# Routed token rows loaded in 32-token blocks and turned by VectorE instead of TensorE

## The reference

```python
sort_idx = jnp.argsort(sel_flat)
xs = x_exp[sort_idx]
group_sizes = jnp.bincount(sel_flat, length=E).astype(jnp.int32)
g = jax.lax.ragged_dot(xs, w_gate, group_sizes)
u = jax.lax.ragged_dot(xs, w_up, group_sizes)
d = jax.lax.ragged_dot(jax.nn.silu(g) * u, w_down, group_sizes)
...
out = d[unsort_idx].reshape(T, K, H)
expert_out = jnp.sum(out * weights[..., None], axis=1)
shared = jax.nn.silu(x @ sw_gate) * (x @ sw_up) @ sw_down
```

## Time and profile before

| what | us |
|---|---|
| median of 3 runs | 2290.17 (2286.09 to 2292.93) |
| span of the profiled execution | 2293.4 |
| TensorE busy | 1971.3 (86%) |
| VectorE busy | 1182.9 (52%) |
| ScalarE busy | 565.1 (25%) |
| GpSimd busy | 1116.9 (49%) |

### The profile page before, as it was taken

One profiled execution on the slowest core, in us unless ns is written; L12 is line 12 of the kernel. 1 busy time (PEld: TensorE's weight loads), 2 busy tenths in 40 slices (PEclk: granted clock), 3 DMA queues, 4 the chain that ended last, 5 costly groups with the idle time before them and its releaser, 6 DMA issues. The chain is left out here.

```text
span 2293.4 us, 33594 instructions
## 1 busy us (share of the span) xinstructions
PE 1971.3 (86%) x10564; PEld 1441.9 (63%) x10565; DVE 1182.9 (52%) x2230; ACT 565.1 (25%) x1164; POOL 1116.9 (49%) x552
## 2 busy tenths in 40 slices
PE   5956887968896689998799999999999999997991
PEld 3423443743343233333599989999999999996880
DVE  2554443557776767774774335444444455443330
ACT  3320222401114345443222212121212121211110
POOL 0000000003457356564044558666666788777886
PEclk9977998888996789999899999999999999998995
DMA  3043101402225366711135445545445555654999
GB/s 116 0 112 105 46 27 44 158 32 85 83 71 186 133 213 211 230 52 43 40 105 182 170 142 165 168 151 170 154 150 167 183 163 178 193 165 118 209 202 211
DMA packets 199487, 305.98 MB, mean 133 GB/s; under 512 B 16472, under 2 KB 94808, under 8 KB 199416
## 3 DMA queue, kind: packets, MB, share of 16 engines
q1 hardware_dynamic: 141624, 187.24, 26.0%
q0 software_dynamic: 21504, 50.93, 9.6%
q10 hardware_dynamic: 36288, 66.84, 8.2%
HBM read 186.42 MB, written 118.55 MB: 133 GB/s over the span
## 5 line engine op out<-in xcount | busy, mean ns | idle before, releaser
L2456 PE MATMUL psum<-e_gu_high,e_rowT_high 128*128 (+1 forms) x1272 | 430.5, 341 | 22.3 <-POOL e_gu_low L2111 14.0
L2456 PE MATMUL psum<-e_gu_low,e_rowT_high 128*128 (+1 forms) x1272 | 410.3, 324 | 0.0
L2180 ACT ACTIVATE e_silu<-psum 128x352 f32<-128x352 f32 x159 | 73.9, 465 | 873.2 <-PE psum L2461 847.1
L2456 PEld LDWEIGHTS psum<-e_gu_high,e_rowT_high 128*128 128x128 f32 x1272 | 241.8, 190 | 50.2 <-issue 46.2
L2461 PE MATMUL psum<-e_gu_high,e_rowT_low 128*128 (+1 forms) x1272 | 256.8, 324 | 0.0
L2456 PEld LDWEIGHTS psum<-e_gu_low,e_rowT_high 128*128 128x128 f32 x1272 | 242.8, 191 | 3.5
L2258 DVE TENSOR_TENSOR e_midT_low<-psum,e_midT_high 128x256 fp32r<-128x256 f32 x159 | 67.5, 424 | 341.1 <-ACT e_midT_high L2189 326.1
L2461 PEld LDWEIGHTS psum<-e_gu_high,e_rowT_low 128*128 128x128 f32 x1272 | 214.5, 190 | 0.0
L2476 PE MATMUL psum<-e_d_high,e_midT_high 128*128 (+3 forms) x477 | 188.0, 394 | 1.0 <-ACT e_midT_high L2189 1.0
L2476 PE MATMUL psum<-e_d_low,e_midT_high 128*128 (+3 forms) x477 | 188.5, 395 | 0.0
L2107 POOL TENSOR_TENSOR e_gu_high<-f_gu_in,e_ones 128x1408 fp32r<-128x1408 f32 x31 | 78.6, 2534 | 198.1 <-PE psum L2461 181.8
(11 more groups left out here) (380 smaller groups left out, 3950.6 us busy)
## 6 DMA issues: line engine op xcount, KB each, us to landing
d_sorted<-f_hs SPq DMA_DIRECT2D x32, 1048.0 KB, 10.4
e_row<-d_sorted ACTq DMA_DIRECT2D x125, 262.0 KB
d_y<-f_arena ACTq DMA_DIRECT2D x127, 256.0 KB
f_gu_in<-in_L_ffn_w_gate SPq DMA_DIRECT2D x32, 704.0 KB, 5.2
f_gu_in<-in_L_ffn_w_up SPq DMA_DIRECT2D x32, 704.0 KB, 5.1
f_d_in<-in_L_ffn_w_down SPq DMA_DIRECT2D x32, 512.0 KB
d_y<-f_hs SPq DMA_DIRECT2D x8, 1024.0 KB, 5.8
f_d_in<-in_L_ffn_w_down SPq DMA_DIRECT2D x32, 192.0 KB
```

The costliest lines, as they stand in the source:

```text
L2456: nc.tensor.matmul(bank[:, 0:M].unsqueeze(1), rowT_high[par][:, k, :], w[:, bass.ds(buffer, 1), k, at:at + M], start=(k == 0 and n == 0), ...
```

## The change

`turn_row` remains for the shared tiles alone; the routed rows reach XT another way.

A routed tile is 128 tokens by 512 features. It is now loaded by four DMAs, one for each quarter of the features (`load_row`): quarter r goes to partitions 32r to 32r+31, and the four blocks of 32 tokens lie side by side in each partition, 128 features of each. A fifth DMA brings the twelve routing numbers of each token into a tile of their own, `side`. VectorE turns the 32x32 blocks of the tile in one instruction (`turn_blocks`), reading with a stride of four numbers and writing to XT. The result has feature 4p+k in partition p, place k, instead of feature 128k+p, so the gate and up weights of the routed experts are loaded in the same order (`"(p k) n"`). ScalarE's copy and VectorE's low part read XT with patterns that undo the order of the token blocks (`copy_blocks`, `low_blocks`). Their places in the lists change: `copy_blocks(i+1)` stands ahead of `silus(i)` on ScalarE, behind the row DMAs; `turn_blocks(i+2)` stands between `multiply(i)` and `copy_y(i-1)` on VectorE and waits for the DMAs of row tile i+2; `load(i)` also waits for `blocks_turned`. In the last shared tile TensorE no longer waits for the first routed rows.

```diff
+BLOCK = 32
...
-        row = [sbuf(nc, stack, f"e_row{n}", [P, ROW]) for n in range(2)]
+        row = [sbuf(nc, stack, f"e_row{n}", [P, D]) for n in range(2)]
+        side = [sbuf(nc, stack, f"e_side{n}", [P, 2 * TOPK]) for n in range(2)]
...
+        sorted_blocks = c.dram["d_sorted"].rearrange("(t n b) d -> b t n d", n=P // BLOCK, b=BLOCK)
...
+        def load_row(eng, tile, par):
+            for r in range(P // BLOCK):
+                eng.dma_start(row[par][r * BLOCK:(r + 1) * BLOCK, :].rearrange("b (n q) -> b n q", n=P // BLOCK).unsqueeze(1),
+                              sorted_blocks[:, tile, :, r * P:(r + 1) * P]).then_inc(row_loaded[par], 16)
+            eng.dma_start(side[par][:].unsqueeze(1), sorted_tiles[:, tile, D:ROW]).then_inc(row_loaded[par], 16)
+        LANDED = 16 * (P // BLOCK + 1)
...
-            def load(n, gate, up, down):
+            def load(n, order, gate, up, down):
...
-                sp.dma_start(gu_in[:, :, 0:M], gate.rearrange("(k p) n -> p k n", p=P)).then_inc(gate_loaded, 16)
+                sp.dma_start(gu_in[:, :, 0:M], gate.rearrange(order, p=P)).then_inc(gate_loaded, 16)
...
-                sp.dma_start(gu_in[:, :, M:2 * M], up.rearrange("(k p) n -> p k n", p=P)).then_inc(up_loaded, 16)
+                sp.dma_start(gu_in[:, :, M:2 * M], up.rearrange(order, p=P)).then_inc(up_loaded, 16)
...
-                load(n, c.dram["L1_ffn_sw_gate"][:, half], c.dram["L1_ffn_sw_up"][:, half], c.dram["L1_ffn_sw_down"][half, :])
+                load(n, "(k p) n -> p k n", c.dram["L1_ffn_sw_gate"][:, half], c.dram["L1_ffn_sw_up"][:, half], c.dram["L1_ffn_sw_down"][half, :])
...
-                load(e + 2, *(c.dram[w][bass.ds(e, 1)].rearrange("a k n -> (a k) n")
+                load(e + 2, "(p k) n -> p k n", *(c.dram[w][bass.ds(e, 1)].rearrange("a k n -> (a k) n")
...
-                sp.dma_start(row[par][:].unsqueeze(1), sorted_tiles[:, par:par + 1, :]).then_inc(row_loaded[par], 16)
+                load_row(sp, slice(par, par + 1), par)
...
-                act.dma_start(row[par][:].unsqueeze(1), sorted_tiles[:, bass.ds(i + 2 - SHARED_TILES, 1), :]).then_inc(row_loaded[par], 16)
+                act.wait_ge(blocks_turned, i - SHARED_TILES + 1)
+                load_row(act, bass.ds(i + 2 - SHARED_TILES, 1), par)
...
+            def copy_blocks(i, par):
+                act.wait_ge(blocks_turned, i - SHARED_TILES + 1)
+                act.wait_ge(up_done, i - 1)
+                nc.scalar.copy(rowT_high[par][:].rearrange("p k (n b) -> p k n b", b=BLOCK),
+                               XT.rearrange("p (n k b) -> p k n b", k=CC, b=BLOCK)).then_inc(rowT_high_ready, 1)
...
-            def steps(i, par, loads=False, stores=False, old=True, more=True):
+            def steps(i, par, loads=False, stores=False, old=True, more=True, blocks=True):
...
+                if more and blocks:
+                    copy_blocks(i + 1, 1 - par)
...
-                if more:
+                if more and not blocks:
...
-            for i in range(NT + 2, SHARED_TILES):
-                steps(i, i % 2)
+            for i in range(NT + 2, SHARED_TILES - 1):
+                steps(i, i % 2, blocks=False)
+            steps(SHARED_TILES - 1, 1, more=False)
+            copy_blocks(SHARED_TILES, 0)
...
+            def turn_blocks(i, par, loads):
+                dve.wait_ge(rowT_low_ready, i)
+                dve.wait_ge(row_loaded[par], LANDED * loads)
+                nc.vector.transpose(XT.rearrange("p (n k b) -> p n k b", k=CC, b=BLOCK),
+                                    row[par][:].rearrange("p (n b k) -> p n k b", k=CC, b=BLOCK)).then_inc(blocks_turned, 1)
+            def low_blocks(i, par):
+                dve.wait_ge(rowT_high_ready, i + 1)
+                nc.vector.tensor_tensor(rowT_low[par][:].rearrange("p k (n b) -> p k n b", b=BLOCK),
+                                        XT.rearrange("p (n k b) -> p k n b", k=CC, b=BLOCK),
+                                        rowT_high[par][:].bitcast(F32).rearrange("p k (n b) -> p k n b", b=BLOCK),
+                                        ALU.subtract).then_inc(rowT_low_ready, 1)
...
-                nc.vector.scalar_tensor_tensor(picked[par][:], row[par][:, D + TOPK:ROW], expert, row[par][:, D:D + TOPK],
+                nc.vector.scalar_tensor_tensor(picked[par][:], side[par][:, TOPK:2 * TOPK], expert, side[par][:, 0:TOPK],
...
-                low_rowT(i + 1, (i + 1) % 2)
-                if i + 1 == SHARED_TILES:
-                    take_weight(i + 1, (i + 1) % 2)
+                if i + 1 < SHARED_TILES:
+                    low_rowT(i + 1, (i + 1) % 2)
...
-            def routed_steps(i, par, more=True):
+            def routed_steps(i, par, more=True, loads=None):
...
-                    low_rowT(i + 1, 1 - par)
+                    low_blocks(i + 1, 1 - par)
...
+                if loads is not None:
+                    turn_blocks(i + 2, par, loads)
...
-            routed_steps(SHARED_TILES, 0)
+            turn_blocks(SHARED_TILES, 0, 1)
+            low_blocks(SHARED_TILES, 0)
+            take_weight(SHARED_TILES, 0)
+            turn_blocks(SHARED_TILES + 1, 1, 1)
+            routed_steps(SHARED_TILES, 0, loads=2)
...
-                routed_steps(i, i % 2)
+                routed_steps(i, i % 2, loads=(i - SHARED_TILES) // 2 + 2)
...
-                    routed_steps(n * 2 + par, par)
+                    routed_steps(n * 2 + par, par, loads=n - SHARED_TILES // 2 + 2)
...
-                routed_steps(i, i % 2, more=(i + 1 < TILES))
+                routed_steps(i, i % 2, more=(i + 1 < TILES), loads=((i - SHARED_TILES) // 2 + 2 if i + 2 < TILES else None))
...
-            def turn_row(i, par, loads=None):
-                if loads is not None:
-                    pe.wait_ge(row_loaded[par], loads)
-                source = hs[:, i % NT, :] if loads is None else row[par][:]
+            def turn_row(i):
...
-                    last = nc.tensor.transpose(XT[:, k * P:(k + 1) * P], source[:, k * P:(k + 1) * P], c.ident[:])
+                    last = nc.tensor.transpose(XT[:, k * P:(k + 1) * P], hs[:, i % NT, k * P:(k + 1) * P], c.ident[:])
...
-                if more:
-                    turn_row(i + 1, 1 - par, loads)
+                if turns:
+                    turn_row(i + 1)
...
```

More of the change, by code:

```diff
@@ L2036, in routed_ffn @@
             nc, c, "e_", "gate_loaded up_loaded down_loaded arrivals_seen high_ready gate_split up_split down_split")
-        row_turned, rowT_high_ready, rowT_low_ready, gate_done, up_done, silu_ready, mid_ready, mid_turned = sems(
-            nc, c, "e_", "row_turned rowT_high_ready rowT_low_ready gate_done up_done silu_ready mid_ready mid_turned")
+        row_turned, blocks_turned, rowT_high_ready, rowT_low_ready, gate_done, up_done, silu_ready, mid_ready, mid_turned = sems(
+            nc, c, "e_", "row_turned blocks_turned rowT_high_ready rowT_low_ready gate_done up_done silu_ready mid_ready mid_turned")
         midT_high_ready, midT_low_ready, down_done, y_copied = sems(
@@ L2219, in _ @@
             for i in range(NT + 2):
-                steps(i, i % 2, old=(i > 0))
+                steps(i, i % 2, old=(i > 0), blocks=False)
                 if SECOND_SPLIT <= i < SECOND_SPLIT + 3:
@@ L2486, in set_of, with tile @@
                 return pe.value_load(tile_set[0:1, bass.ds(i - SHARED_TILES, 1)], min_val=2, max_val=E_ + 1)
-            def tile(i, par, e, old, more=True, loads=None, used=None, before=None, also=None):
+            def tile(i, par, e, old, turns=False, used=None, before=None, also=None):
                 pe.wait_ge(rowT_high_ready, i + 1)
@@ L2508, in shared_tile @@
             def shared_tile(i, also=None):
-                tile(i, i % 2, i // NT, (i - 1) // NT if i > 0 else None, loads=(16 if i + 1 == SHARED_TILES else None),
+                tile(i, i % 2, i // NT, (i - 1) // NT if i > 0 else None, turns=(i + 1 < SHARED_TILES),
                      used=(i - 1 if i >= 2 else None), before=(i - 2 if i >= 3 else None), also=also)
-            turn_row(0, 0)
+            turn_row(0)
             shared_tile(0)
@@ L2523, in _ @@
                 shared_tile(i, also=table_ready)
-            tile(SHARED_TILES, 0, set_of(SHARED_TILES), 1, loads=16, used=SHARED_TILES - 1, before=SHARED_TILES - 2)
-            tile(SHARED_TILES + 1, 1, set_of(SHARED_TILES + 1), set_of(SHARED_TILES), loads=32, used=SHARED_TILES, before=SHARED_TILES - 1)
+            tile(SHARED_TILES, 0, set_of(SHARED_TILES), 1, used=SHARED_TILES - 1, before=SHARED_TILES - 2)
+            tile(SHARED_TILES + 1, 1, set_of(SHARED_TILES + 1), set_of(SHARED_TILES), used=SHARED_TILES, before=SHARED_TILES - 1)
             with pe.Fori(SHARED_TILES // 2 + 1, LOOP_END) as n:
-                tile(n * 2, 0, set_of(n * 2), set_of(n * 2 - 1), loads=16 * (n + 1 - SHARED_TILES // 2), used=n * 2 - 1, before=n * 2 - 2)
```

(6 more changed lines are left out.)

## The result

The changed kernel takes 2276.6 us (median, 2276.1 to 2276.8) against 2289.8 for the kernel before: a ratio of 0.994, with a 95% interval of 0.993 to 0.996. It is faster by 13 us. I had forecast 34 us, so the direction held and the size did not.

The account below looks back on a forecast made before the run. TensorE was taken to bound the routed tiles, GpSimd's gathers the end. From the profiled span, 2293.4 - 43.0 - 2 + 3 + 8 = 2259.4, so 2256 as median; forecast 2243 to 2270 (0.72), stated range 2243 to 2283.

Parts of the forecast that it names:

- the first rival: DMA pieces cost by their number: 3.3 us more a row load, 46 us behind 2118, no change at 2294; chance 0.07.
- What bounds the kernel: TensorE sets the pace up to 2031 us; behind it GpSimd's own list does, where a faster tile gains nothing.
- What the turn costs TensorE: The four transposes cost TensorE 0.43 us a routed tile; without them 6.26 us, 43.0 us over 100 tiles.
- What moves on ScalarE: Five row loads behind take_weight make SiLU 1.1 us late; TensorE waits 0.1 us in such tiles, 3 us in all.
- VectorE's turn: The block transpose on VectorE takes 0.68 us, bounds 0.58 and 2.7; VectorE is not the bound.
- GpSimd and the turn: VectorE's turn reads one SBUF operand, so by the shared-port rule GpSimd does not hold it up: free.
- The second rival: VectorE's block transpose waits for GpSimd as take_weight does: 61 us slower, 2351; chance 0.07.
- The row's arrival: Row loads land 4.4 us after issue, before VectorE asks; TensorE is hit only from an arrival of 8.7 us on.
- The start: TensorE no longer waits for the first routed row in the last shared tile: 2 us gained, bounds 0 and 4.
- The gathers: Smaller row-load pieces compete with GpSimd's gathers behind 2118: 0.91 us more a load, 8 us lost, bounds 0 and 12.7.

Follow-up runs that it names:

- the kernel with both moves: Changed kernel with the table reads and loop's branch ahead of the wait in down, and row DMAs freed from take_weight: 2238.0 us (0.978).
- the kernel before with its reads moved: Kernel before, with TensorE's two table reads and the loop's branch moved ahead of the wait in down: 2285.5 us (0.9985).
- The experiment with the reads moved in either kernel: Table reads and loop's branch moved ahead of the wait in down: 2257.2 us in the changed kernel, 2285.5 us in the kernel before.
- the third read: Changed kernel with a third, unused table read at the head of each tile of the loop: 2313.8 us (1.011 to before).

## Why the prediction was wrong in size

The measured 2276.6 us lies where I had put a part of the first rival's price (2270 to 2283). That is luck: that rival did not come, and the time was lost at another place.

- **What bounds the kernel: right.** TensorE in the middle, GpSimd's list from the first gather on. Between the two profiled executions the end moved by 18.5 us, the first gather by 16.0.
- **What the turn costs TensorE: right as work, wrong as time.** Taken alone it is worth 0.37 us a tile, and 0.47 where the sequencer has room before and after (6.74 to 6.27, the kernel with both moves against the kernel before with its reads moved). The 0.43 of the earlier trace rows is in between. The changed kernel kept 0.12 of it, 98 x 0.12 = 12 us.
- **What moves on ScalarE: the step that failed.** The lateness was right, 1.0 us against 1.1, and also how many tiles have it, 26 of 95 against "about a third". What failed is "1.0 us is left. TensorE so waits 0.1 us in such a tile". I measured `copy_midT`'s slack up to `down`'s first weight load. Even up to there it is short: in the late tile the load starts at 1453.07, 0.38 after `copy_midT` ends, and late tiles wait 0.31 at `down` on the mean. But above all TensorE's sequencer needs that result before it can go on with its own list, 3.3 us up to the next gate product, and `down`'s weight loads cover 1.9 of it. A late tile loses 0.79 us against one on time (7.21 and 6.43), 20 us in all, where I had 3. And "TensorE has no other wait" was wrong for the rest: the tiles on time take 6.43 instead of 6.33 (6.76 - 0.43), another 10 us. In the kernel before, the four transposes were 0.43 us of cover for this list, so that it showed for 0.17 us a tile; the 6.69 that I took for a tile is one without that gap, and the mean was 6.76. The experiment with the reads moved in either kernel shows it: 2 us before the change, 19 after it.
- **VectorE's turn: wrong in size, without effect.** 1.10 us where I took 0.68; the bounds (0.58 to 2.7) held. Without the stride it is 0.72, so the row that I chose was right for the instruction and not for its pattern. VectorE is at 65 of 100.
- **GpSimd and the turn: right.** The turn took 1.11 us beside GpSimd's step of 1448.64 in the late tile above, and 1.08 to 1.12 in all 127 cases. The second rival did not come, as the shared-port rule in "SBUF — State Buffer" (SBUF: two separate sides) of the Trainium skill had it; by this trace it holds for this instruction.
- **The row's arrival: right.** The turn waits for DMAs 4.0 us in all tiles together, seven times (first row: count, shortest/median/longest ns, first and last start; second: idle us ahead of it, times):

```profile
L2277 DVE STREAM_TRANSPOSE psum<-e_row x127: 1080/1099/1120, 1344.7 to 2208.6; 128x512 f32<-128x512 f32 x127
...
  DMA e_side<-d_sorted: 4.0, 7
```

- **The start: 2 forecast, 0.3 between the two profiled executions** (13.95 to 13.61 us from the last shared SiLU to the first routed one). TensorE waited 4.56 us for the row there, and now waits 3.18 for `copy_blocks` in front of the first routed tile; behind the wait it ran for a while at the lower of its two clocks (1.2 GHz, not 2.4), with a granted clock from 1345 to 1352 of 0.52 before and 0.76 after. But the term stays open, because the stretch hangs on when GpSimd's scatter ends. The first row DMA was issued 2.08 us behind the last shared SiLU in the one execution and 1.47 behind it in the other. Where it was issued ahead of that SiLU, the stretch took 8.3 us in the kernel before with its reads moved, and 10.4 to 10.5 in the kernels without the stride, with both moves and with the third read. By these the changed start may even be the longer one.

```profile
1345.00:1352.00 7.00, 5.24 (x18) 5.10 (x19) 1.33 (x4) 0.59 (x1) 0.43 (x1) 0.52 0.35 115
```

```profile
1345.00:1352.00 7.00, 5.18 (x23) 5.11 (x24) 5.32 (x5) 0.59 (x1) 7.00 (x3) 0.76 0.22 39
```

- **The gathers: wrong sign.** I took +8 for the smaller pieces; the 87 gathers took 3.2 us less. Over all runs they take 162.8 to 163.3 us in the three kernels with the old loads and 159.6 to 162.0 in the six with the new ones; why they are shorter was not tried. The load of small pieces raised ScalarE's queue from 22.9% to 27.2% of 82 us, 3.5 us of all engines for some 11 loads, 0.3 each where I had 0.91. The first rival, with 46 us, is refuted: gathers are 1.86 us apart. A packet of ScalarE's queue took 0.272 x 82 x 16 / 9973 = 36 ns, near the 38 of the earlier trace rows. The 48-byte pieces that I weighed by "DMA: Bandwidth & Descriptors" (Specifications) of the Trainium skill cannot be told from the rest here, but no such price shows.

The sum of the profiled executions, 18.5 us at the last gather, with measured terms: 12 in the tiles, 0.3 at the start, 2.5 in the gathers. A further 2.5 us lie ahead of the change, since the last shared SiLU already came that much earlier, and some 1.1 between the last tiles counted and the first gather. The medians differ by 13 because the profiled execution of before took longer than its median run: a run's time is 1.7 us above its span (2276.6 and 2274.9 for the profiled run of the changed kernel), so the span of 2293.4 stands for 2295.1, some 5.3 above the median of before.

## What to carry to other kernels

An engine that is busy all the time can hide the time its own sequencer needs; before work is taken from it, count the sequencer's instructions (table reads, branches, address work, waits) from the last wake-up to the next matmul against the work still queued. A slack has to be read up to the sequencer that waits, not up to the instruction that the timeline shows behind the wait. And reads that depend on nothing belong ahead of a wait in which the engine stands anyway: here that, with the row DMAs taken out of a chain, made 13 us into 49.

## What the runs showed of the hardware

A table read by TensorE's sequencer took 0.30 us in most tiles, and 0.64 to 0.75 up to the start of what follows its register work, but up to 0.72 by itself in the changed kernel and 1.14 in the kernel before:

```profile
L2525 PEldq TENSOR_LOAD <-f_tile_set x166: 294/301/723, 1400.2 to 1946.1; - x166
```

```profile
L2486 PEldq TENSOR_LOAD <-f_tile_set x162: 295/306/1137, 1405.4 to 1946.9; - x162
```

All 11 over 0.4 us in the changed kernel, and 40 of 62 before, lay across VectorE's change from the low part to `take_weight`; what holds them was not tried and stays open. A block transpose of 128x512 fp32 numbers from SBUF to PSUM took 0.72 us with neighbouring numbers and 1.10 us with a read stride of four, and all 127 turns of the changed kernel lay within 1.08 to 1.12, GpSimd busy beside them or not.
